# Two streams of a eight-layer network on one core: waits merged into their instructions' turns, and new turn tables

## What is computed

```python
x = x + _L0_attn_ref(_layernorm(x, axis=-1), ...)   # state space: conv, 16 heads, norm, projection
x = x + _L0_ffn_ref(_layernorm(x, axis=-1), ...)    # token-mixing feed-forward
x = x + _L1_attn_ref(_layernorm(x, axis=-1), ...)   # Mamba: 256 channels, 16 states
x = x + _L1_ffn_ref(_layernorm(x, axis=-1), ...)    # 8 experts, top 2, gelu
x = x + _L2_attn_ref(_layernorm(x, axis=-1), ...)   # linear attention, 16 heads
x = x + _L2_ffn_ref(_layernorm(x, axis=-1), ...)    # ternary feed-forward, 128-512-512-512-128
x = x + _L3_attn_ref(_layernorm(x, axis=-1), ...)   # state scan with input-dependent decay
x = x + _L3_ffn_ref(_layernorm(x, axis=-1), ...)    # 8 experts, top 2, silu gate
```

## Time and profile before

| | us |
|---|---|
| median of 3 timed runs | 1424.91 |
| lowest and highest | 1422.25, 1425.74 |
| span of the profiled execution | 1400.6 |
| TensorE busy in it | 1104.8 |
| VectorE busy | 890.9 |
| ScalarE busy | 630.4 |
| GpSimd busy | 281.7 |

### The profile page before, as it was taken

How to read it: one execution, slowest core, us unless ns; L and a number is a source line. 1 busy time by engine, 2 the same in 40 slices (tenths; PEclk the granted TensorE clock), 3 DMA queues, 4 the chain that set the end, 5 groups by cost and what they waited for, 6 DMA issues and landing times.

```text
span 1400.6 us, 15057 instructions
## 1 busy us (share of the span) xinstructions
PE 1104.8 (79%) x4959; PEld 698.7 (50%) x4959; DVE 890.9 (64%) x1919; ACT 630.4 (45%) x1194; POOL 281.7 (20%) x258
## 2 busy tenths in 40 slices
PE   4978657767977979686768676799999899897791
PEld 2536312334743634353457442574555556787781
DVE  6787879987558767767635789723735652363432
ACT  3433385424552348634237972273252434542330
POOL 3000113324120002130230244202000032014404
PEclk9999877777989999878889897999999999899996
DMA  8100000003520000000125420370000014468782
GB/s 322 47 0 1 0 0 0 0 1 118 163 61 1 0 0 1 0 0 0 45 92 177 131 74 21 96 224 21 1 1 0 1 63 132 157 214 283 260 277 69
DMA packets 49411, 107.02 MB, mean 76 GB/s; under 512 B 4840, under 2 KB 32368, under 8 KB 48688
## 3 DMA queue, kind: packets, MB, share of 16 engines
q1 hardware_dynamic: 44656, 92.74, 20.7%
q0 software_dynamic: 4096, 8.40, 2.0%
q10 hardware_dynamic: 576, 4.87, 0.8%
HBM read 91.24 MB, written 14.75 MB: 76 GB/s over the span
## 4 chain that ended last, share of the span: by engine, by line
PE 41%; DVE 22%; ACT 13%; issue 9%; POOL 7%; DMA 6%; SPq 1%; DVEq 0%; POOLq 0%; ACTq 0%
PE ps L1920 6%; PE ps L1638 5%; DMA expert_ring<-in_e_dram 4%; PE ps L1586 4%; PE ps L1752 4%; DVE up L1341 3%; PE ps L1858 3%; POOL slots_dram L717 3%; ACT big L957 2%; PE ps L1692 2%; PE ps L1829 2%; PE ps L1958 2%; DVE big L1348 2%; POOL up L727 2%; PE ps L1909 1%
## 5 line engine op out<-in xcount | busy, mean ns | idle before, releaser
L1858 PE MATMUL ps<-big,expert_ring 128*128 128x128 f32 x1160 | 158.0, 286 | 33.6 <-DMA expert_ring<-in_e_dram 20.4
L1858 PEld LDWEIGHTS ps<-big,expert_ring 128*128 128x128 f32 x1160 | 145.2, 199 | 48.0 <-DMA expert_ring<-in_e_dram 26.9
L1341 DVE TENSOR_TENSOR_SCAN up<-cv,big 128x512 f32<-128x512 f32 x128 | 152.5, 1230 | 21.5 <-ACT cv L908 17.4
L660 POOL TENSOR_TENSOR rstd<-ve,nhalf 128x4 f32<-128x4 f32 (+1 forms) x41 | 47.2, 1153 | 577.2 <-DVE ve L1119 470.6
L1752 PE MATMUL ps<-big,consts 128*128 128x512 f32 x256 | 154.3, 735 | 2.4 <-DVE big L1348 2.4
L697 POOL TENSOR_TENSOR big<-big,mt 128x512 f32<-128x512 f32 x64 | 85.8, 1344 | 279.1 <-ACT mt L901 152.6
L1920 PE MATMUL ps<-big,weights 128*128 128x512 f32 x256 | 115.4, 597 | 0.0
L1769 PE MATMUL ps<-q,row_pick 96*128 96x512 bf16 x128 | 54.5, 448 | 76.6 <-DVE big L1348 61.4
L1829 PE MATMUL ps<-expert_ring,big 128*128 128x128 f32 x792 | 107.6, 280 | 5.9 <-ACT big L957 3.6
L1829 PEld LDWEIGHTS ps<-expert_ring,big 128*128 128x128 f32 x792 | 98.9, 195 | 15.3 <-ACT big L957 9.8
L1459 DVE SCALAR_TENSOR_TENSOR big<-ps,expert_ring,key 128x128 f32<-128x128 f32 x184 | 51.8, 344 | 79.6 <-PE ps L1858 67.4
(11 more groups left out here) (247 smaller groups left out, 1943.4 us busy)
## 6 DMA issues: line engine op xcount, KB each, us to landing
expert_ring<-in_e_dram SPq DMA_DIRECT2D x46, 836.0 KB, 5.3
expert_ring<-in_e_dram SPq DMA_DIRECT2D x53, 578.0 KB, 4.4
big<-slots_dram SPq DMA_DIRECT2D x21, 256.0 KB, 3.5
results_dram<-mt SPq DMA_DIRECT2D x21, 256.0 KB, 5.3
weights<-in_w_dram ACTq DMA_DIRECT2D x1, 3072.0 KB, 15.5
slots_dram<-big SPq DMA_DIRECT2D x2, 1024.0 KB, 10.3
weights<-in_w_dram SPq DMA_DIRECT2D x1, 1600.0 KB, 8.6
x<-in_x_dram SPq DMA_DIRECT2D x4, 256.0 KB, 13.6
```

Source lines behind the costliest of these rows:

```text
L1341: dve.tensor_tensor_scan(UP[s][:, j, PAD:PAD + T], CV[s][:, j, :], BIG2[s][:, j, :], 0.0, ALU.mult, ALU.add).then_inc(m_scan[s], 1)
L1858: last = pe.matmul(bank4(s, r if m else b % 2)[:, k, :], ring[:, q % RING, r * T + k * P:r * T + (k + 1) * P], XGT[s][:, b // 4 % 4, b % 4 ...
```

## The change

Waits that stood between two `yield`s, in turns without an instruction, are moved into the turn of the instruction that needs them, and one `yield` that only followed a wait is made conditional (seven places in all). Each generator then has fewer turns (TensorE's tables count 1237 turns before and 1121 after, VectorE's 903 and 839; ScalarE's and GpSimd's 704 and 239 both times), and all five tables in `RUNS` are new. The tables of SyncE and two of the waits, from the diff:

```diff
     "sp": [
-        1, 1, 23, 35, 57, 7, 1, 6, 1, 4, 1, 20],
+        0, 1, 24, 35, 56, 1, 1, 2, 1, 8, 1, 11, 1, 15],
...
                     dve.tensor_tensor(BIG2[s][:, 0, :], bank(s, 2), BIG1[s][:, 2, :], ALU.mult).then_inc(m_scan[s], 1)
-                    yield
-                    dve.wait_ge(m_scan[s], m_scan.at(s, 4 * n))
                     for j in range(2):
                         yield
+                        if j == 0:
+                            dve.wait_ge(m_scan[s], m_scan.at(s, 4 * n))
                         dve.wait_ge(m_da[s], m_da.at(s, 2 * n + j))
...
                 def turn_block(s, j):
-                    yield
-                    if j >= 2:
-                        pe.wait_ge(l0_yn[s], l0_yn.at(s, j - 2))
                     for c in range(NC):
                         yield
+                        if c == 0 and j >= 2:
+                            pe.wait_ge(l0_yn[s], l0_yn.at(s, j - 2))
                         if j == 0:
                             pe.wait_ge(l0_nm[s], l0_nm.at(s, c))
```

More of the change, by code:

```diff
@@ L140 @@
     "pe": [
[11 rows of a table removed]
-    "act": [
[8 rows of a table removed]
-    "dve": [
[11 rows of a table removed]
[12 rows of a table added]
+    "act": [
[9 rows of a table added]
+    "dve": [
[11 rows of a table added]
     "pool": [
-        1, 1, 1, 1, 1, 1, 1, 1, 1, 1, 2, 2, 4, 1, 2, 1, 2, 1, 2, 1, 2, 1, 2, 1, 2, 2, 1, 2, 8, 8, 9, 3, 1,
-        9, 1, 4, 1, 1, 1, 1, 1, 17, 1, 2, 14, 3, 1, 3, 1, 4, 1, 4, 1, 2, 1, 1, 9, 1, 10, 3, 1, 1, 18, 19,
-        16, 16],
+        0, 2, 3, 1, 1, 1, 1, 1, 2, 2, 4, 2, 2, 1, 1, 1, 3, 1, 2, 1, 4, 2, 1, 2, 8, 8, 9, 2, 1, 9, 1, 5, 1, 1,
+        2, 16, 1, 4, 13, 1, 1, 3, 1, 2, 1, 2, 1, 6, 1, 2, 1, 1, 9, 1, 10, 3, 1, 1, 18, 19, 16, 16],
     "sp": [
-        1, 1, 23, 35, 57, 7, 1, 6, 1, 4, 1, 20],
+        0, 1, 24, 35, 56, 1, 1, 2, 1, 8, 1, 11, 1, 15],
 }
@@ L1755, in mamba @@
                 for n in range(NM):
-                    yield
-                    if n == 0:
-                        pe.wait_ge(m_mix[s], m_mix.at(s, 0))
-                        pe.wait_ge(m_sp[s], m_sp.at(s, 1))
                     for k in range(2):
                         yield
+                        if n == 0 and k == 0:
+                            pe.wait_ge(m_mix[s], m_mix.at(s, 0))
+                            pe.wait_ge(m_sp[s], m_sp.at(s, 1))
                         if n and k == 0:
@@ L1904, in ternary @@
                     for r, name in enumerate(("t_w1", "t_w2")):
-                        yield
+                        if j or r:
+                            yield
                         if j >= 2:
@@ L1911, in ternary @@
                 for name, p, src in (("t_h1", t_p1, 0), ("t_h2", t_p2, 4)):
-                    yield
-                    if src == 0:
-                        pe.wait_ge(t_h0[s], t_h0.at(s, 3))
                     for j in range(4):
@@ L1917, in ternary @@
                             yield
+                            if src == j == b == 0:
+                                pe.wait_ge(t_h0[s], t_h0.at(s, 3))
                             if src:
```

## The result

| | before | changed |
|---|---|---|
| median of 11 timed runs, us | 1422.88 | 1429.97 |
| lowest to highest | 1418.96 to 1433.12 | 1422.96 to 1433.89 |
| ratio, 95% interval | | 1.0043 (1.0022 to 1.0063) |
| span of the profiled execution | 1400.6 | 1428.1 |

The changed kernel is slower by 0.43%, some 6 us, where 0.4% faster was forecast.

What follows compares the result with a forecast made beforehand. No engine is full throughout; order wins only where a full engine idles or one stream's chain stands behind the other. 0 + 0 - 1 - 1.5 - 3.5 = minus 6: span 1394.6, plus 24.3 gives 1419 us, range 1408 to 1430.

Steps and rivals of the forecast that it cites:

- The time around the span: Timed median 1424.9 us minus profiled span 1400.6: 24.3 us taken to lie outside the span and held fixed.
- Merged waits 0: Waits merged into their instructions' turns, whole kernel: 0 us, since no TensorE instruction goes and each stream keeps its order.
- The Mamba stretch 0: 170 to 300 us, both streams in the Mamba layer, VectorE full: reordering changes 0 us, bounds minus 11 to plus 5.
- idle near 11: Sign of being right: VectorE's idle time in the Mamba stretch stays near 11 us.
- hundreds of other places: Places across the kernel where single groups changed sides: no row prices them, they only widen the main forecast's range.
- Table loads -1: ScalarE: five fewer table loads, 6.4 us less work, 13% of it on the chain: minus 1 us, bounds 0 and 6.4.
- Heads of queues -1.5: VectorE at 417.38 and 672.53, GpSimd at 828.70 us: ready work goes first, minus 1.5 us, bounds 0 and 7.7.
- The tail -3.5: Way into stream 1's last expert layer and the tail after it: minus 3.5 us, bounds plus 3 to minus 10.
- Displacements (2) to (4): Before stream 1's last layer: transposes to second logits 2.4 us less, ranking product 3.9 less, VectorE's start on ranks 0.6 less.
- my d: What stream 0 loses in the tail by standing behind stream 1: 0 to 3.6 us, taken as 1.
- Rival D: VectorE's queue in the tail: stream 0's weighted sums wait for late gathers, slower, 1431 us; chance 0.18.
- my signs of being wrong: Time before 1200 us moves over 5 us; TensorE's idle before stream 1's first block stays near 5; stream 0's last block over 3 later.

Runs made afterwards that it cites:

- e2: Merged waits alone, with tables keeping the instruction order of the kernel before on all engines; ratio 0.9995 to the kernel before.
- e14: Merged waits, old order, only ScalarE's moves from 762 to 791 us new; 176.1 us from 700 to 870 us, against 170.4 to 171.2 in the old order.
- e6: Merged waits, new order from 702 to 870 us alone, old order elsewhere; ratio 1.0062 to the kernel before, 8.7 us slower.
- e5: Merged waits, new order from 318 to 702 us alone, old order elsewhere; ratio 0.9972 to the kernel before, 3.9 us faster.
- e7: Changed kernel with the old order back at 150 to 318 and 702 to 870 us; ratio 0.9922 to the kernel before, 10.9 us faster.
- e4: Merged waits, old order up to 1110 us, new order behind it; ratio 0.9984 to the kernel before, 2.3 us faster.
- e3: Merged waits, new order up to 318 us, old order behind it; ratio 1.0066 to the kernel before, 9.4 us slower.
- e11: Merged waits, new order from 762 to 791 us alone on TensorE, ScalarE and VectorE; 177.1 us from 700 to 870 us, old order 171.1.
- e13: Merged waits, old order, only VectorE's moves from 762 to 791 us new; 177.0 us from 700 to 870 us, against 170.4 to 171.2 in the old order.

## Why the prediction was wrong, step by step

*The time around the span.* 24.3 us were held fixed as lying outside; only about 2 us lie there, the rest is the stall (about 25 us) that this execution did not have. It would have cost nothing in a difference, had the stall not touched the very place of the forecast.

*Merged waits 0.* Right (e2).

*The Mamba stretch 0: the step that failed.* "Moving work inside a full engine exchanges who finishes first and leaves the sum." The sum did not stay: 5.3 us more, just over my upper bound of 5, which I had reasoned from another mechanism; that the number is near is luck. I checked for VectorE's idle time and took a scan's 1.2 us as a constant. Idle stayed small from 216 to 283 us, 0 before and 2.4 after, but the scans grew from 1208 to 1268 ns. The rows to read were GpSimd's, for when its product and a scan run at once. My sentence on what would show it (idle near 11) was the wrong test: the loss is as much in the busy time.

*The second Mamba layer.* Not in the sum at all, save that a table load and GpSimd's idle 3.27 us at 828.70 were counted as gains there. It holds the larger loss, 8.4 us. It is the "hundreds of other places" that had "no row that prices them"; the order did show one of them (an add of the other stream between two scans that stood together). TensorE's clock, which is 0.83 there instead of 0.87, stood in none of my terms.

*Table loads -1.* The five went, and ScalarE has 9.6 us less to do (6.4 of them table loads). What they are worth no run shows by itself: e14 moved activations without saving a load and lost 5.4 us, and e6, with two loads fewer, lost 8.7 with all else that changed in its stretch. A saved load and a copy made late came in the same table, and I had priced only the first.

*Heads of queues -1.5.* Sign right, size too small by the middle value: 3.9 us from 318 to 702 us by e5 (0.8 to 7.0, so 1.5 isn't excluded), inside my bounds of 0 to 7.7. That stretch holds two of the three heads; GpSimd's at 828.70 is in the stretch that lost.

*The tail -3.5.* -3.9 in the one trace without the stall (e7), -1.0 with it, and -2.3 (-5.5 to +1.1) by e4's timed runs. The size came by other steps than mine. The first scatter of e7, and of the changed kernel, beside the earlier trace rows:

```profile
1254.93 1.03 POOL L718 DMA_INDIRECT slots_dram<-cv,key  x1 [15.63 <-DVE key L1403]
```

```profile
1257.75 1.03 POOL L718 DMA_INDIRECT slots_dram<-cv,key  x1 [15.03 <-DVE key L1403]
```

From the scan's last product (line 1954 at 1219.85 and 1222.17) that is 35.1 and 35.6 us, before 38.8: 3.2 to 3.7 us earlier and not 8 to 12. Displacements (2) to (4) lie in this span and were priced at 6.9 us; half of it came. Which of them failed I did not take apart. Then SyncE's and TensorE's timelines of e7, beside the earlier trace rows:

```profile
1277.87 0.43 SPq L642 DMA_DIRECT2D results_dram<-mt  x1
1280.94 0.34 SPq L630 DMA_DIRECT2D expert_ring<-in_e_dram  x1
1281.32 0.44 SPq L638 DMA_DIRECT2D big<-slots_dram  x1
1284.27 0.38 SPq L642 DMA_DIRECT2D results_dram<-mt  x1
1284.69 1.64 SPq L638 DMA_DIRECT2D big<-slots_dram  x3
```

```profile
1286.88 1.12 PE L1810 MATMUL ps<-consts,big 128*128 128x128 f32 x4 [2.97 <-DMA big<-slots_dram]
```

```profile
1288.38 0.98 POOL L728 DMA_INDIRECT up<-results_dram,key  x1 [13.48 <-DMA results_dram<-mt]
```

The order store, then loads two to four, is as I wrote, and TensorE's wait for the tokens is 2.97 instead of 4.97 us. But the first load, sent at 1281.32, stands behind a weight load that waits for a block of stream 0, so the first block starts 67.0 us after the scan's product, before 66.0: a loss of 1 where I had a gain of 1.8 to 2.5. Stream 0's last block ends 3.0 us later (my d, taken as 1). What wins is the gathers: they start 68.5 us after the product instead of 75.0. Two us of that is the store (64.4 after the product instead of 66.4); the rest is that it lands after 4.1 us instead of 8.5. It no longer stands behind four token loads and a weight load, which I take for the reason; no run moved the store alone. I had counted only when it is sent. The sums after it wait less, beside the earlier trace rows, in e7's timeline of VectorE (after: no wait at all at its first sum, 1327.76):

```profile
1298.60 1.14 DVE L1433 SCALAR_TENSOR_TENSOR x<-up,key,x 128x128 f32<-128x128 f32 x4 [1.50 <-DMA up<-results_dram,key]
```

I had expected 3 us or more there. *Rival D* (slower by those sums) is excluded by the same row. *With the stall* the scatters and the stalled loads decide: scatter to first block is 45.0 to 45.6 us in three traces with the new tail and 39.0 to 39.6 in four with the old, so the earlier scatter is taken back. Why the new order stalls longer there is open.

*What came out slower* was thus none of my rivals, but one of my signs of being wrong came, that the time before 1200 us moves by more than 5. The product that begins at 1110.1 us in before begins at 1111.9 in the changed kernel; in the three other traces with the old order throughout up to there it begins at 1101.5, 1105.2 and 1103.6, so the mean of the four is 6.8 us earlier. The timed parts add up to +9.4 (e3) - 3.9 (e5) + 8.7 (e6) - 2.3 (e4) = +11.9 us, each with some 3.3 us of uncertainty; the change measured +6 (3 to 9). The 6 us between them are inside these uncertainties, and the parts may also not add up, as in e11. The stretch from 870 to 1110 us is in none of the four parts.

## What to carry to other kernels

- A full engine's time is not fixed under a reordering: look for instructions whose duration varies in the trace (their largest beside their mean), and at what the engine that shares a port with it does then. Put the collision on the engine that has time to spare.
- An instruction of another stream put between two that ran in one piece costs whenever its operand comes later than the second one's; read that from the trace for each such place before pricing the place at zero. Before counting a table load saved on ScalarE (1.28 us), look at which copies the new order makes late and whether TensorE waits for one of them.
- When two profiles differ by several times what the timed runs do, find the stretch in which they part before reading anything else, and profile the unchanged kernel again. The same holds for a stretch: two traces of one order differed by 3 us there after a weight load came late.

## What the runs showed of the hardware

- VectorE's scan with both inputs in SBUF and GpSimd's product exclude each other for the whole instruction, whichever starts second: scans of 1.20 us took up to 2.22 us beside a product (before, at 213.84), a GpSimd product of 0.20 us took 0.97.
- During GpSimd's 16 scatters and again during its 16 gathers the loads that SyncE issues stood still for up to 17.5 us at a time (9.7 or more at least once) in 9 of 16 traces and for 3.7 at most in the other 7, the program of before among both; it made 25 us of 1420. What decides it is open; no run here was made to find out.
- A wait of 1.29 us on TensorE, with 0.80 and 0.53 us just before it, was followed by a granted clock of 0.51 for 10 us (e14); with 0.64 and 0.70 us and no third wait it stayed at 1.00 for the same work (e2). A wait of 2.25 us for weights (e13) and one of 1.82 (e3) were followed by 0.79 over 8 us, where e2, with 0.30 us, had 1.00.
